# A fixed text for TensorE's order in causal attention, in place of a greedy planner

## The reference

```python
scores = jnp.einsum('bhqd,bhkd->bhqk', q, k) * SCALE
causal = jnp.tril(jnp.ones((s, s), dtype=bool))
scores = jnp.where(causal, scores, -jnp.inf)
weights = jax.nn.softmax(scores, axis=-1)
out = jnp.einsum('bhqk,bhkd->bhqd', weights, v)
```

## Time and profile before

| | |
|---|---|
| median of 3 runs | 2121.22 us (2119.86 to 2122.55) |
| profiled execution, its own time | 2130.2 us |
| its span | 2128.5 us |
| mean granted TensorE clock | 0.977 of full |
| TensorE busy | 2024.1 us, 95% of the span |
| VectorE busy | 1830.4 us, 86% |
| ScalarE busy | 1346.9 us, 63% |
| GpSimd busy | 249.2 us, 12% |

### The profile page before, as it was taken

One profiled execution on the slowest core, in us unless ns is written; L12 is line 12 of the kernel. 1 busy time (PEld: TensorE's weight loads), 2 busy tenths in 40 slices (PEclk: granted clock), 3 DMA queues, 4 the chain that ended last, 5 costly groups with the idle time before them and its releaser, 6 DMA issues.

```text
span 2128.5 us, 39561 instructions
## 1 busy us (share of the span) xinstructions
PE 2024.1 (95%) x15696; PEld 860.9 (40%) x15696; DVE 1830.4 (86%) x3611; ACT 1346.9 (63%) x1637; POOL 249.2 (12%) x349
## 2 busy tenths in 40 slices
PE   6998999999999999999999999999999995899997
PEld 3665333333333333333333333333333323667664
DVE  6877999999899989998998999899899926799883
ACT  3665357777777777777777777777777781333332
POOL 3000001010111001010110101011100104222000
PEclk9999789999999999999999999999999997999999
DMA  3898212240504133150404225040413024544320
GB/s 116 246 275 253 60 32 51 42 87 8 86 16 78 39 59 71 24 86 7 87 20 79 55 41 85 7 87 13 81 43 57 12 93 100 137 113 121 94 65 30
DMA packets 143755, 162.53 MB, mean 76 GB/s; under 512 B 52178, under 2 KB 117970, under 8 KB 143570
## 3 DMA queue, kind: packets, MB, share of 16 engines
q1 hardware_dynamic: 136658, 147.39, 29.8%
q0 software_dynamic: 6912, 12.61, 2.7%
HBM read 99.90 MB, written 59.77 MB: 75 GB/s over the span
## 4 chain that ended last, share of the span: by engine, by line
PE 74%; DVE 17%; ACT 4%; DMA 2%; issue 1%; SPq 1%; POOL 0%; ACTq 0%; POOLq 0%; DVEq 0%
PE b_psO L1034 23%; PE b_psS L1017 20%; PE b_ring L998 16%; DVE b_pmax L920 6%; PE a_psQK L562 3%; PE c_psH L1397 3%; PE b_ring L996 3%; PE c_psO L1410 2%; DMA a_x<-in_L_attn_x 2%; PE a_psV L572 1%; ACT b_prob L958 1%; DVE c_attn L105 1%; PE c_psA L1367 1%; DVE c_inv L477 1%; DVE c_ln_f_stats L81 1%
## 5 line engine op out<-in xcount | busy, mean ns | idle before, releaser
L920 DVE TENSOR_REDUCE b_pmax<-b_ring 128x1 f32<-128x512 f32 (+4 forms) x2336 | 1360.6, 648 | 91.9 <-PE b_ring L998 80.6
L958 ACT ACTIVATE b_prob<-b_psS 128x1024 f32<-128x1024 f32 (+3 forms) x1280 | 1083.1, 896 | 416.9 <-PE b_psS L1017 409.5
L1017 PE MATMUL b_psS<-g_qT,g_kT 33*128 33x512 bf16 (+7 forms) x5120 | 773.9, 349 | 4.1 <-ACT b_prob L958 2.7
L998 PE MATMUL b_ring<-g_kT,g_qT 64*128 64x512 bf16 (+3 forms) x2560 | 673.4, 354 | 5.6 <-DVE b_pmax L920 3.7
L1034 PE MATMUL b_psO<-b_prob,g_v 128*32 128x512 f32 (+3 forms) x5120 | 595.3, 541 | 1.8 <-POOL b_prob L910 1.8
L1017 PEld LDWEIGHTS b_psS<-g_qT,g_kT 64*128 64x128 bf16 (+1 forms) x5120 | 306.5, 94 | 164.1 <-ACT b_prob L958 55.6
L998 PEld LDWEIGHTS b_ring<-g_kT,g_qT 64*128 64x128 bf16 x2560 | 196.6, 94 | 426.3 <-DVE b_pmax L920 369.1
L910 POOL TENSOR_SCALAR_AFFINE_SELECT b_prob<-b_prob 128x512 f32<-128x512 f32 x256 | 163.1, 637 | 1572.4 <-ACT b_prob L958 1572.4
L996 PE MATMUL b_ring<-later,query_of 64*128 64x128 bf16 x1024 | 180.9, 225 | 9.6 <-DVE b_pmax L920 7.1
L996 PEld LDWEIGHTS b_ring<-later,query_of 64*128 64x128 bf16 x1024 | 82.0, 94 | 223.5 <-DVE b_pmax L920 189.1
L1034 PEld LDWEIGHTS b_psO<-b_prob,g_v 128*32 128x32 f32 x5120 | 103.6, 108 | 165.2 <-issue 132.2
(11 more groups left out here) (96 smaller groups left out, 999.0 us busy)
## 6 DMA issues: line engine op xcount, KB each, us to landing
qk_parts<-a_parts SPq DMA_DIRECT2D x64, 384.0 KB, 4.4
g_qT<-qk_parts SPq DMA_DIRECT2D x192, 128.0 KB, 4.4
g_kT<-qk_parts SPq DMA_DIRECT2D x192, 128.0 KB, 4.2
out_sums<-b_outT SPq DMA_DIRECT2D x64, 256.0 KB, 3.1
v_ones<-a_v SPq DMA_DIRECT2D x16, 544.0 KB, 5.8
g_v<-v_ones SPq DMA_DIRECT2D x32, 272.0 KB, 4.0
a_x<-in_L_attn_x SPq DMA_DIRECT2D x16, 512.0 KB, 5.7
c_x<-in_L_attn_x SPq DMA_DIRECT2D x16, 512.0 KB, 7.3
```

Of the source, the lines that this page charges most:

```text
L920: nc.vector.tensor_reduce(pmax[:, c % 2].rearrange("p (h t) n -> p h t n", t=TT)[:, heads[0]:heads[-1] + 1:2, qt, pc], ring[:, r % BANKS, ...
L958: nc.scalar.activation(prob[:, j % PBUF, 2 * s:2 * s + 2, off:CH], psS[:, 2 * s:2 * s + 2, off:CH], ACT.Exp).then_inc(exp_done, 1)
L998: ins_ = nc.tensor.matmul(to, qT[own, g, h // 2, 0, t * P:(t + 1) * P], kT[own, g, h // 2, 0, pc * CH:pc * CH + w], start=pc < c, stop=Tru ...
L1017: ins_ = nc.tensor.matmul(psS[:, 2 * s + p, off:CH], kT[own, g, s, ab, kt * P:(kt + 1) * P], qT[own, g, s, ab, c * CH + off:(c + 1) * CH], ...
```

## The change

The class `Plan` goes. In its place stands `ORDERS`, a text of 8160 signs, one for each piece: `0` and `1` are the next score product of that half, `a` and `b` the next unit whose first head is on half 0 or 1, `t` the next turn, `v` the next values. `read_orders` turns it into the same kind of list as before, with the same fields; `first` and `last` are worked out as before. Nothing else changes: stage A, stage C, the bodies of the engines in stage B, buffers, banks and semaphores are the same lines.

```diff
-class Plan:
-    MODE, SEEN, TURNED, PLACED = 95, 198, 500, 4600
-    READ, MASKED, LOOK = 64, 840, 6
...
-ORDER = Plan().order
+ORDERS = (
+    "aaaaaababbabbbbbtbabbbababbb01010101ab1a0b0a11100ba1v1a1100ab10ab01v1a1000a0aavvbtbbbaaaaaaa0101a10a01b0"
+    "b011b1010bbva1010b10b01ava1010b0101abv1a10b01ba001b010bb10101bbvab01011a1v1ab0000a0aavab0vt111bbbvbaaaaa"
...
+    "a0101av0b010b011a1avb0b0a1vba100bb1b1bv0b1a10tbbabbbaaava1111000a0a1010100ba1v0101aa0101abvb01a01a1010bv"
+    "t1a1a1010b0b0v1a0b01a1010bv1a10ab10100bv0b01ba10101av0b01ab0101a1v1a100bb0101ava10b0101a10bvb00b0101b1a1"
...
+    "10101a1a000011t0101v10110v0101010v1010010110101010v1010v0101v01011010v01011010v01011010v1010v10101010v01"
+    "01v10101010v1010010101010101v0101v01010101v1010010101011010v01011010v01011010v1010vvv",
+)
+def read_orders():
+    jobs = max_jobs()
+    units_of = [[n for n, job in enumerate(jobs) if job[0] == "max" and job[6][0] % 2 == p] for p in range(2)]
+    turns = [n for n, job in enumerate(jobs) if job[0] == "turn"]
...
+    for sign in "".join(ORDERS):
+        if sign in "01":
+            p = int(sign)
+            j, rest = divmod(at[p], 4)
+            s, ab = divmod(rest, 2)
+            assert j - valued < PBUF and left[KEY_STEPS[j][:3]] == 0
+            order.append(("scores", j, s, ab, p, at[1 - p] <= at[p] and ab == 0, at[1 - p] > at[p] and ab == 1))
+            at[p] += 1
+        elif sign in "ab":
...
+            order.append((*job, left[job[1:4]] == 0))
+        elif sign == "t":
...
+            assert left[job[1:]] == 0
+            order.append(job)
         else:
...
+            assert min(at) >= 4 * (valued + 1)
+            order.append(("values", valued))
+            valued += 1
+ORDER = read_orders()
```

More of the change, by code:

```diff
@@ new lines, in read_orders @@
+def read_orders():
+    jobs = max_jobs()
+    units_of = [[n for n, job in enumerate(jobs) if job[0] == "max" and job[6][0] % 2 == p] for p in range(2)]
+    turns = [n for n, job in enumerate(jobs) if job[0] == "turn"]
+    left = {}
+    for job in jobs:
+        if job[0] == "max":
+            left[job[1:4]] = left.get(job[1:4], 0) + 1
+    order, at, taken, turned, valued = [], [0, 0], [0, 0], 0, 0
+    for sign in "".join(ORDERS):
[7 more added lines that the diff above has]
+        elif sign in "ab":
+            p = "ab".index(sign)
+            job = jobs[units_of[p][taken[p]]]
+            taken[p] += 1
+            left[job[1:4]] -= 1
+            order.append((*job, left[job[1:4]] == 0))
+        elif sign == "t":
+            job = jobs[turns[turned]]
+            turned += 1
+            assert left[job[1:]] == 0
+            order.append(job)
+        else:
+            assert min(at) >= 4 * (valued + 1)
+            order.append(("values", valued))
+            valued += 1
+    assert valued == len(KEY_STEPS) and turned == len(turns) and not any(left.values())
+    return order
```

210 lines of the change are left out of this document (74 added, 136 removed).

## The result

| | before | after |
|---|---|---|
| median of 4 runs each | 2120.92 us | 2087.39 us (2082.12 to 2088.1) |
| ratio, 95% interval | | 0.9836 (0.9819 to 0.9853) |
| profiled execution, its own time | 2130.2 us | 2087.79 us |
| its span | 2128.5 us | 2086.1 us |
| end of the attention in it | 1757.9 us | 1725.8 us |

A forecast was written before the change was run, and what follows sets the result against it. TensorE and VectorE were taken as equally loaded, the bound changing by stretch. Savings of 38 (middle), 3 (first iteration) and 5 (last), less 1 for late turns, made 45 us: from the median 2121.2 to 2076 us, range 2050 to 2102.

The forecast's parts named there:

- first iteration, and the stretch ahead of it: Start of the attention: its first chunks still wait for VectorE, which the order hardly moves; 3 us less.
- last iteration, up to the release of the next stage: Steps 560 to 615 were to save 5 us; the last 24 steps, paced by ScalarE, nothing.
- What bounds the kernel: Attention: TensorE and VectorE equally loaded, the bound changing by stretch; a full step takes the larger, 2.49 against 2.38 us.
- nearly all waits go: Rival, 13%: the middle comes within 1% of TensorE's own 1064.7 us, saving 60, the ends 12; whole 2050 us.
- The count of the middle: Six middle iterations, larger of the two engines between values: 1096.3 us against a measured 1134.5, so 38.2 us less.
- The interpolation of 21%: Middle iterations: the old period lies 21% up from the count by pairs to that by single sections; the new likewise.
- The excess of VectorE over TensorE: Middle sections: VectorE's surplus over TensorE, summed where positive, was to fall from 82.0 to 54.8 us.
- Same-half neighbours: Rival about consecutive pieces on one half: full blocking at 0.16 us each, 2148 us, 5%; load's price, about 2119, 4%.
- Leads of three or four: At 132 of 5120 score products, one half's scores run further ahead; cost 0, between -3 and +5 us.
- Late turns: Seven chunks whose row of maxima may return after their first scores are due: 0 to 5 us, taken as 1 lost.
- The offset of the profiled execution: Whole kernel: the profiled execution's own time was put 9 us above the median of the runs shown.
- Tail within 1 us: Sign for the last 24 steps, scores and values only: their time was to stay within 1 us.

The follow-up runs named there:

- The searched start: Against the order with the planner's first 44 steps and a searched rest, the first 44 and last 40 steps searched as well: 2060.68 us, ratio 0.9707.

## Why the prediction was right, and where not

The terms of its sum, against the profiled executions:

| term | forecast | measured |
|---|---|---|
| six middle iterations, with the late turns | -38.2 + 1 | -36.5 |
| first iteration, and the stretch ahead of it | -3 | +9.4 - 0.5 |
| last iteration, up to the release of the next stage | -5 | -7.1 + 1.7 |
| sum | -45.2 | -33.0 |

These are the differences up to the release of the next stage. The medians of the whole kernels differ by 33.5. One term was wrong, and it is nearly the whole difference of 12 us.

**What bounds the kernel: right.** Two engines equally loaded, and an order that loses what one has to spare where the other is short. The kernel with units alone moved shows it: the same pieces, only evened out, and 22 us less, as counted. Two readings beside it were off. The 30 middle sections without a unit, in which VectorE was to starve, include 18 that hold nothing and take 0.46 us each, and those 18 are the ones that the new order keeps. And the 63.5 us of VectorE's waits left out the 18.7 before the turns' copies, which the count priced alike in both orders (0.4 us for a copy with its wait). The rival "nearly all waits go" did not come: the middle's 1098.0 us lie 33 above TensorE's own 1064.7.

**The count of the middle: right.** 1098.0 against 1096.3, and then for three further orders 1112.1 against 1113.1, 1138.5 against 1133.6 and 1084.9 against 1086.7. The interpolation of 21%, fitted to one number, held for all of these to 0.5%. It failed wholly where units were bunched (1238.6 against 1084.5). That it would hold was luck in so far as both orders of the change have their units spread; the prediction did not name that condition. The excess of VectorE over TensorE, given as 82.0 and 54.8, does not fit the table above it: the sum by sections less TensorE alone is 73.0 and 43.4. It falls by about as much and enters no term. One figure inside it was wrong: values of 128 columns do not take at least 0.42 us. In the TensorE timeline of after the next piece begins 0.36 behind them, the 0.145 for the change of pieces included:

```profile
454.06 0.42 PE L1000 MATMUL b_psO<-b_prob,g_v 128*32 128x128 f32 x8
454.42 0.23 PE L962 MATMUL b_ring<-later,query_of 64*128 64x128 bf16 x1
```

Both orders have the same values, so the difference between them hardly suffered.

**Same-half neighbours: right.** The exclusion rested on one row; the kernel with 2527 such neighbours measures the price as zero, 189.07 against 189.08. By the Trainium skill (TensorE: Matmul & The Clock Gate, The mechanism) a weight load overlaps a matmul in flight only when it goes to other rows of the array; the measurement here decides against it for these pieces: 64-row tiles followed one another on one half at no cost. The same section also lets a load go ahead of matmuls in flight when it targets a background weight buffer, which would fit; no run here shows which it was.

**Leads of three or four: right**, cost zero (the kernel that cuts them back is 0.6 us shorter in its middle).

**Late turns: not separated.** The fourth middle iteration takes 184.8 against 182.2 to 183.1 for the rest, but the text has 297 units between its first values and its last there, and 289 to 294 in the others: five units more at 0.60 are 3 us. So there is no room for late rows of maxima in it. In the waits of after, none of TensorE's names a transfer; but the four transfers of a row have no landing in the trace, and 52 waits of the scores' weight loads, 20.0 us in all and at most 0.8, have no releaser ("issue", shown above), where before has none of this kind. So no score waited a microsecond for a row, and the 1 us cannot be told from nothing. No run moved turns alone.

**The first iteration: wrong**, -3 forecast, +9.4 measured. The step that failed is "its first chunks still wait for VectorE, and that the order hardly moves". I took the 0.90 of its window as a given of both kernels, and counted TensorE's columns at the full clock. At half clock a stream takes twice its time (values of step 0 last 1.93 instead of 1.07), TensorE's side of each section doubles, and an order that is even at the full clock is not even there. This row is the start of after:

```profile
229.69 1.93 PE L1000 MATMUL b_psO<-b_prob,g_v 128*32 128x512 f32 x8
```

And how long the half clock lasts was itself not the same in the two orders, on average by 13 us. The searched start shows that this stretch depends on the order: step 80 begins at 441.9.

**The last iteration:** the sum was right by two errors that cancel. Up to step 616 it gained 2 more than forecast, and the tail was not "nothing": 46.0 against 43.4, since the new mixture of whole and half steps leaves ScalarE gaps of 0.35 to 0.57 us where the old one has 0.33, as in this row of after:

```profile
1707.58 5.75 ACT L924 ACTIVATE b_prob<-b_psS 128x1024 f32<-128x1024 f32 x6 [0.57 <-PE b_psS L983]
```

1.7 of these 2.6 lie ahead of the release. That release I had put to eight steps before the end because a loop counts so; it is the storing of the chunk that ends with the values of step 623.

**The offset of the profiled execution: right in size, its place left unsaid.** I subtracted 9 us from the profiled time to reach the median. Against the profile of after, the profile of before is 9.3 us longer in the stage after the attention (398.8 against 389.5), and so the offset most likely lies there; a profile of before at its median time, which would show it, does not exist.

Of the signs, the reciprocals 182 to 184 us apart and unequal (182.2 to 184.8), ring waits 30 to 40 (38.1), VectorE at 94 to 95% (95), clock 1.00 in the middle: all as said. "Tail within 1 us" was not (2.6).

## What to carry to other kernels

Where two engines are both loaded above 90% and one is fed by the other through a few buffers, count the work of both between two fixed events (here two values) for the order at hand: the sum of the larger of the two is the period, and with a share of borrowing fitted to one order it was right to 0.5% and mostly to 0.2%, as long as the pieces that feed the other engine are spread over their section and do not come in bunches larger than the buffers hold. An order fixed for one speed of an engine must be priced at the other speed too, for the stretches in which the granted clock is low; a text for the start and one for the middle are two problems. And two profiles are compared between release points first: what differed from one execution to the other in a stage that the change does not touch was a fifth of the difference here. Where every execution's span and mean clock are on record, they tell a low clock that belongs to a kernel from one that belongs to an execution.

## What the runs showed of the hardware

- The granted clock at the attention's start was at half for 44 to 72 us in total, in executions of the same first 40 steps too (44.4 and 71.7), while from 335 us on it stayed at the full level to the end of the attention in every profile here. 18 transposes, 2.2 us in a gap of 4.5 us of TensorE at that start, put its beginning off by 4.5 us and left its end and the iteration's time as they were.
- Over whole executions, 28 with the new start had 103 us at half clock on average and 54 with the planner's had 90; 1 us more at half clock went with 0.43 us more time among executions of one kernel.
- 2075 more score products and units that follow one on the same half: no time at all (189.07 against 189.08 us for an iteration).
- Entering and leaving values costs the same whether a unit or a score follows: 1.00 us from values to the next piece in the earlier trace rows, and 1.00 in the step shown of after.
